# Every third step's edge rows and every fourth step's mask made in the first edge pass, and the softmax's copies on ScalarE

## The reference

```
# weighted layer
neighbor = segment_sum(weight * x[src], dst)
out = x @ W1.T + b1 + (neighbor + neighbor * x) @ W2.T + b2
x = layernorm(x + normalize(leaky_relu(out, 0.2)))
# attention layer: two convolutions of 4 heads of 64 channels, relu between them
q, k, v = h @ Wq + bq, h @ Wk + bk, h @ Wv + bv
e = edge_attr @ We
logits = sum_c(q[dst] * (k[src] + e)) / sqrt(64)
a = softmax of logits over the edges of one dst
conv = segment_sum((v[src] + e) * a, dst) + h @ Ws + bs
x = layernorm(x + conv2(relu(conv1(x))))
```

## Time and profile before

| what | value |
|---|---|
| median of 3 runs | 4665.41 us |
| the profiled execution, its own time | 4668.24 us |
| its span, first to last instruction | 4666.5 us |
| mean granted TensorE clock | 0.981 of full |
| TensorE (PE) busy | 4159.3 us, 89% |
| VectorE (DVE) busy | 3873.8 us, 83% |
| ScalarE (ACT) busy | 2969.4 us, 64% |
| GpSimd (POOL) busy | 3113.8 us, 67% |
| DMA, mean | 214 GB/s, 996.73 MB |

### The profile page before, as it was taken

One profiled execution on the slowest core, in us unless ns is written; L12 is line 12 of the kernel. 1 busy time (PEld: TensorE's weight loads), 2 busy tenths in 40 slices (PEclk: granted clock), 3 DMA queues, 4 the chain that ended last, 5 costly groups with the idle time before them and its releaser, 6 DMA issues. The chain is left out here.

```text
span 4666.5 us, 107658 instructions
## 1 busy us (share of the span) xinstructions
PE 4159.3 (89%) x17694; PEld 3201.7 (69%) x17694; DVE 3873.8 (83%) x21108; ACT 2969.4 (64%) x10607; POOL 3113.8 (67%) x2996
## 2 busy tenths in 40 slices
PE   2888888888978999999999998979999999999989
PEld 2766666665546777777777775557777777777755
DVE  4655555556869999999999998879999999999987
ACT  1111111112316999999999996129999999999970
POOL 6677777770038777777777772188777877787730
PEclk9999999998999999999999999999999999999999
DMA  4666666664558888888888884578888888888844
GB/s 117 189 195 193 193 195 193 193 187 132 167 174 258 241 245 248 244 244 243 245 248 243 248 241 127 181 227 243 243 239 241 239 243 243 240 241 242 241 124 155
DMA packets 663064, 996.73 MB, mean 214 GB/s; under 512 B 99667, under 2 KB 489690, under 8 KB 662407
## 3 DMA queue, kind: packets, MB, share of 16 engines
q0 software_dynamic: 171408, 540.40, 39.3%
q1 hardware_dynamic: 491000, 449.44, 31.8%
HBM read 870.01 MB, written 119.44 MB: 212 GB/s over the span
## 5 line engine op out<-in xcount | busy, mean ns | idle before, releaser
L1303 POOL DMA_INDIRECT e_kv<-kv,src x1664 | 1633.9, 982 | 599.1 <-DVE e_kvj L1418 289.5
L1558 ACT ACTIVATE e_vals<-e_kvj,e_ex 128x65 f32<-128x65 f32 x6572 | 1723.2, 334 | 1.3 <-PE e_sum L1366 1.3
L1325 PE MATMUL e_q<-q,e_pick 128*128 x3328 | 1035.1, 392 | 146.4 <-DVE e_logit L1430 111.4
L1430 DVE CUSTOM_DVE_ANT_0 e_kvj<-e_kvj,e_q 128x64 f32<-128x64 f32 x6656 | 1062.5, 214 | 7.6 <-PE e_q L1325 2.7
L1366 PE MATMUL e_sum<-e_vals,e_mask 128*128 128x260 f32 x3328 | 1033.6, 393 | 28.7 <-ACT e_vals L1558 15.3
L152 POOL DMA_INDIRECT e_x<-x_rows,e_src x783 | 745.1, 952 | 263.6 <-issue 174.0
L1418 DVE TENSOR_TENSOR e_kvj<-e_kv,e_e 128x512 f32<-128x512 f32 x1248 | 845.5, 678 | 44.3 <-DMA e_kv<-kv,src 39.2
L1325 PEld LDWEIGHTS e_q<-q,e_pick 128*128 128x128 f32 x3328 | 594.1, 191 | 376.4 <-issue 302.0
L1315 PE MATMUL e_e<-e_we,e_ea 112*128 112x256 f32 x2496 | 749.6, 381 | 15.3 <-DMA e_ea<-attr_tiles 14.6
L1316 PE MATMUL e_e<-e_we,e_ea 112*128 112x256 f32 x2496 | 743.5, 379 | 0.0
L1512 DVE TENSOR_TENSOR acc<-acc,e_sum 128x260 f32 x1664 | 693.8, 417 | 32.2 <-PE e_sum L1366 9.3
(11 more groups left out here) (221 smaller groups left out, 3979.2 us busy)
## 6 DMA issues: line engine op xcount, KB each, us to landing
e_ea<-attr_tiles SPq DMA_DIRECT2D x1248, 112.0 KB
edges<-q SPq DMA_DIRECT2D x208, 256.0 KB, 3.1
e_spots<-locals SPq DMA_DIRECT2D x416, 128.0 KB
e_made<-edges SPq DMA_DIRECT2D x416, 128.0 KB
e_kv<-kv,src POOLq DMA_INDIRECT x1664
kv<-n_proj_rows SPq DMA_DIRECT2D x98, 256.0 KB
q<-attr_tiles SPq DMA_DIRECT2D x208, 112.0 KB
n_x<-x_rows SPq DMA_DIRECT2D x98, 128.0 KB
```

The costliest lines, as they stand in the source:

```text
L1303: e.indirect_dma_start(out=kv[:, u, :], out_offset=None, **rows_of(kv_rows, k["src"][:, i:i + 1])).then_inc(kv_got[u], 16)
L1325: e.matmul(pe_q[i % 2][:, 0:D], pick[:, c, at:at + P], rows, start=True, stop=True).then_inc(q_done, 1)
L1430: dot = e.tensor_tensor_reduce(kvj[:, i % 2, h, 0:C], kvj[:, i % 2, h, 0:C], pe_q[i % 2][:, hs], 1.0, 0.0, ALU.mult, ALU.add, logit[:, j % ...
L1558: by_weight = e.activation(vals[:, n % R, h * HV:(h + 1) * HV], kvj[:, 2 + n % NV, h, :], ACT.Copy, scale=ex[:, b % 2, h, r:r + 1])
```

## The change

e0 makes edge rows at every third step (`TRIO` = 3, 277 times for 208) and also, at every fourth step, the plain mask that e1 and e2 need, on ScalarE, and stores it in a DRAM table `masks` (208 of 64 KB). e1 and e2 read the made rows at every third step, make `e` themselves at two of three, and load the mask at every fourth step (below `LATE`) into two buffers instead of making it. To have room, NE is 4 for 5. The copies of pieces 3 and 5 go from VectorE to ScalarE, where they stand at pieces 2 and 4.

```diff
+TRIO = 3
...
+class PlainMasks:
+    def make(self, e, c):
+        n = c * QUAD
+        if c:
+            e.wait_ge(self.made, c)
+        e.activation(self.apart, self.k["iota"][:], ACT.Square, bias=self.k["local"][:, n:n + 1], scale=-1.0).then_inc(self.apart_done, 1)
+        e.wait_ge(self.apart_done, c + 1)
+        if c >= 2:
+            e.wait_ge(self.stored[c % 2], 16 * (c // 2))
+        e.activation(self.masks[c % 2], self.apart, ACT.Relu, bias=self.k["one"][:, 0:1], scale=-1.0).then_inc(self.made, 1)
+
+    def store(self, e, c):
+        e.wait_ge(self.made, c + 1)
+        e.dma_start(self.table[c * P:(c + 1) * P, :], self.masks[c % 2]).then_inc(self.stored[c % 2], 16)
...
             for i in range(T):
-                c = i // QUAD
-                if i % QUAD == 0 and c + edges.AHEAD - 1 < s.quads:
+                c = i // TRIO
+                if i % TRIO == 0 and c + edges.AHEAD - 1 < s.trios:
                     ahead = c + edges.AHEAD - 1
-                    edges.load(e, ahead, tile.at(QUAD * ahead + QUAD - 1))
-                if i % QUAD == 2 and c:
+                    edges.load(e, ahead, tile.at(TRIO * ahead + TRIO - 1))
+                if i % TRIO == 2 and c:
                     edges.store(e, c - 1)
+                if i % QUAD == 2:
+                    plain.store(e, i // QUAD)
...
-                if i % QUAD == 1:
-                    edges.multiply(e, i // QUAD)
+                if i % TRIO == 1:
+                    edges.multiply(e, i // TRIO)
...
         @block.scalar
         def _(e):
-            for c in range(s.quads):
-                edges.copy(e, c)
+            for i in range(T):
+                if i % QUAD == 1:
+                    plain.make(e, i // QUAD)
+                if i % TRIO == 2:
+                    edges.copy(e, i // TRIO)
...
-    NV, NG, NE, R = LAG + 2, 6, 5, 4
+    NV, NG, NE, R = LAG + 2, 6, 4, 4
...
+        def mask_kept(n):
+            return n < LATE and n % QUAD == 0
+        def masks_before(n):
+            return n - -(-n // QUAD)
+        def mask_of(n):
+            return plain[:, n // QUAD % 2, :] if mask_kept(n) else mask[:, n % R, :]
         def mask_made(e, n):
-            if n < LATE:
-                e.wait_ge(masked, n + 1)
+            if mask_kept(n):
+                c = n // QUAD
+                e.wait_ge(plain_got[c % 2], 16 * (c // 2 + 1))
+            elif n < LATE:
+                e.wait_ge(masked, masks_before(n) + 1)
...
+                def load_mask(c):
+                    if c >= 2:
+                        e.wait_ge(summed, (c - 2) * QUAD + 1)
+                    e.dma_start(plain[:, c % 2, :], masks_made[c * P:(c + 1) * P, :]).then_inc(plain_got[c % 2], 16)
...
-                    if at == QUAD - 1 and c + 1 < s.quads:
+                    if at == TRIO - 1 and c + 1 < s.trios:
                         load_made(c + 1)
+                    n = i - LAG + 3
+                    if n >= 0 and mask_kept(n):
+                        load_mask(n // QUAD)
...
-                        last, before = 7 * PACE + 1, 5 * PACE + 1
+                        last, before = 7 * PACE + 1, 4 * PACE + 1
...
                     elif step == 3:
-                        e.wait_ge(ends_up, j + 1)
+                        e.wait_ge(rows_in, 2 * j + 2)
                         if j:
-                            e.wait_ge(outs_done, j)
                             e.wait_ge(across, j)
                             e.wait_ge(history, j)
-                        e.tensor_copy(by_head(row_f[:]), by_head(small[0:1, 0:RW])).then_inc(rows_in, 1)
-                        e.tensor_copy(by_head(row_b[:]), by_head(small[0:1, RW:2 * RW])).then_inc(rows_in, 1)
-                        e.wait_ge(rows_in, 2 * j + 2)
...
                     elif step == 5:
-                        e.wait_ge(across, j + 1)
-                        e.tensor_copy(ends[:], back[:, P:P + 2]).then_inc(ends_down, 1)
...
-                        if n < LATE:
-                            if n:
-                                e.wait_ge(masked, n)
+                        if n < LATE and not mask_kept(n):
+                            if masks_before(n):
+                                e.wait_ge(masked, masks_before(n))
                             e.activation(apart[:], k["iota"][:], ACT.Square, bias=k["local"][:, n:n + 1],
...
+                    elif step == 2:
+                        e.wait_ge(ends_up, j + 1)
+                        if j:
+                            e.wait_ge(outs_done, j)
+                        e.activation(by_head(row_f[:]), by_head(small[0:1, 0:RW]), ACT.Copy).then_inc(rows_in, 1)
+                        e.activation(by_head(row_b[:]), by_head(small[0:1, RW:2 * RW]), ACT.Copy).then_inc(rows_in, 1)
+                    elif step == 4:
+                        e.wait_ge(across, j + 1)
+                        if j:
+                            e.wait_ge(mx_done, j)
+                        e.activation(ends[:], back[:, P:P + 2], ACT.Copy).then_inc(ends_down, 1)
```

64 lines of the change are left out of this document (38 added, 26 removed).

## The result

| what | before | after |
|---|---|---|
| median | 4669.27 us (7 runs, 4661.03 to 4674.04) | 4652.98 us (7 runs, 4650.67 to 4656.75) |
| ratio after to before | | 0.9968, 95% interval 0.9957 to 0.9979 |
| the profiled execution, its span | 4668.24, 4666.5 us | 4656.75, 4654.4 us |

The change makes the kernel faster by 0.3%: little, but the interval stays under 1. The forecast was 4582, or 83 to 87 us less; it came to 16. The result also lies above the upper end of my range, 4645.

The account below looks back on a forecast made before the run. ScalarE was taken to bound e2, VectorE a hair behind, both sharing e1. From 4668.2 us, minus 97 (attention passes) plus 14 (e0) gave 4585; the median being 2.8 lower, 4582, range 4530 to 4645.

Parts of the forecast that it names:

- The reading of the bound: In e2 ScalarE bounds at 44.9 us a batch, VectorE a hair behind; in e1 the two share it.
- I take a third left: Attention passes: VectorE's idle 1.7 (e1) and 1.1 us (e2) a batch falls to 0.5 and 0.3.
- POOL at 1.62 a step, 42.2 a batch: Attention passes: POOL's need, from 1.25 us a gather and 2.74 where a pick stands between two.
- VectorE's busy time: Attention passes: falls by 0.65 us a batch, to 43.8 in e1 and 43.4 in e2.
- The copies: Softmax in e1 and e2: moving three copies saves VectorE 0.65 us a batch and costs ScalarE 0.77.
- The masks and made rows: Attention passes: masks save ScalarE 4.7 us a batch; made rows save TensorE 1.9.
- SP and transfers: Attention passes: masks add 0.10 us a step of transfers; DMA share reaches 0.92 in e1, 0.90 in e2.
- e0: Weighted pass: added products hidden under POOL's gathers except at both ends, 7.2 us each, +14 us; bounds 3 and 40.
- Transfers cap the pace: Rival, attention passes: transfers capped at 260 GB/s, e1 gains only 0.9 us a batch, time 4609; chance 0.15.
- transfers are the limit today: Rival, attention passes: transfers are already full at 245 GB/s, so added bytes cost time, 4773; chance 0.07.
- It does nothing: Rival, whole kernel: masks or copies end up waited for at the same places, 4665; chance 0.03.
- VectorE's waits stay: Rival, attention passes: VectorE is late for its own reasons, only the copies are gained, 4639; chance 0.13.

Follow-up runs that it names:

- half pick: POOL's pick cut to half its width, result not computed: 4605.5 us (0.9870) in the changed kernel, 4639.2 us (0.9947) in the kernel before.
- pick per three steps: The changed kernel with POOL's pick made for three steps at a time instead of four: 4656.8 us, ratio 0.9982.
- the two kernels without overlaps: The changed kernel with picks made per three steps (4656.8 us), or with made rows back at every fourth step (4652.0 us).

## Why the prediction was wrong

**The reading of the bound.** ScalarE as the bound of e2, at 44.9 us a batch, isn't shown. The copies alone give ScalarE work and take it from VectorE, and e2 gets faster by 9 us; my expectation had named a gain of over 10 us in all as the sign that VectorE was the bound. That e2 then stands at 44.8 us a batch (the line that adds starts 580 times in 1000 us), with ScalarE at 0.978, agrees in number. What the runs do show is that the engines stand so close together in e2 that relieving one brings 14 or 16 us and both 55. What the text never compared was how far below the bound the next engine stood, by means.

**The step that failed: "I take a third left", VectorE's idle time of 0.5 us a batch in e1 and 0.3 in e2.** Measured are 0.034 x 45.8 = 1.6 and 0.017 x 44.7 = 0.8, nearly the old 1.7 and 1.1. I had put this time down to ScalarE and TensorE alone. In e2 this goes back to a number beside the sum, what POOL needs; in e1 the cause stays open.

**In e2: POOL at 1.62 a step, 42.2 a batch.** I took 1.25 and 2.74 from rows of single intervals. They are near the shortest that occur: the gather behind a pick takes 1.33 to the next, and one gather in the same stretch of the trace took 1.23 instead of 0.95. In the kernel before, POOL's true slack in e2 was 37 us in 1000 (worked out above), so its need was 963/576 = 1.67 a step, 43.5 a batch. After the change the gathers and picks are longer by 0.022 and 0.090/4 = 0.023, and 1.67 + 0.045 = 1.715 a step is 44.6 a batch, against 44.7 measured. So POOL became e2's bound within 0.3 us of the old one, with VectorE (43.9 busy) 0.8 below it. The half pick brings e2 to 43.7, partly by relieving VectorE too, and the pick per three steps relieves VectorE alone and brings next to nothing. The stretch by overlap is a part of it at most: in the two kernels without overlaps the gathers stay at 1.007 and 1.018, for which I have no cause, and e2 gains little.

**In e1**, where 46 of the 75 us are missing, the idle time stayed as well, and its cause is open; what the waits say is at the end of this section.

**VectorE's busy time** came out at 44.2 and 43.9 for 43.8 and 43.4; the made adds, 8.7 a batch and each longer by 0.040, are 0.35 of that.

**The copies.** Right in sign, and the only part that pays: 30 us (copies moved back) and 28 us (copies alone) for 40 by my sum of 2 x 0.65 x 30.4. ScalarE's price was set too high (0.77 for some 0.3), and that VectorE's shorter chain gives ScalarE back its wait at the exponential was not seen. That new waits on TensorE cost nothing is neither confirmed nor refuted.

**The masks and made rows.** Forecast as the relief of the bound, 57 us in the passes (97 - 40); over the copies alone they bring 1 us there (+4 and -5) and cost 14 in e0. ScalarE did come down, to 0.872 x 45.8 = 39.9 busy a batch, for the 41.0 forecast as its need; the room isn't used, because POOL and VectorE, and in e1 something else, stand right behind it. "One buffer of attributes fewer" was priced at nothing; in e1's window TensorE and its weight loads now wait 4.4 and 9.3 us for attributes, which they didn't before.

**SP and transfers.** Forecast shares 0.92 and 0.90, measured 0.87 and 0.85. Part of that is the pace; by share times pace the new transfers cost 0.87 x 1.761 - 0.83 x 1.773 = 0.06 and 0.85 x 1.718 - 0.81 x 1.736 = 0.05 a step for my 0.10. "The tightest resource" was wrong here: the run with fewer bytes changed nothing. (The added bytes come to 17.7 kB a step, not 17.6.) For these masks I had an estimate of 0.24 a step from the table of the Trainium skill (DMA: Bandwidth & Descriptors, Bandwidth), whose rows are for transfers issued from GpSimd, while SP loads the masks. The trace doesn't bear the estimate out: the whole change of share is worth 0.05 to 0.06.

**e0.** Right: +10 for +14, with 400 gathers in 500 us as before, and POOL's stop, as I had worked out (26), in the timeline:

```profile
148.79 0.94 POOL L153 DMA_INDIRECT e_x<-x_rows,e_src  x1 [25.65 <-PE e_sum L631]
```

**The rivals.** "Transfers cap the pace" and "transfers are the limit today" fall by the run with fewer bytes. "It does nothing", 4665, came nearest in time, but the interval of the ratio rules it out, and the copies do bring something. "VectorE's waits stay", 4639, was the nearest in mechanism (POOL was named there among others), but it still credited the change with the copies' whole 40 us and saw no lengthening. I gave it 0.13; its argument "POOL already waits for VectorE 89.5 us" I read as POOL following with room, where 52 of the 89.5 were the gap that stands between any two gathers.

**What stays open**: what holds e1 at 45.5 to 46.3 us a batch in nearly every kernel on the first kind of chip. It isn't the amount of bytes (fewer bytes: the same) and not POOL's width (half pick: 8 us). In e1's window POOL waits for VectorE 78.7 us, 174 times, so 26.5 over the gaps. VectorE's largest waits there are these:

```profile
DVE e_block_rows L469 <- PE e_back L461: 13.2, 28, 0.9
DVE e_kvj L1478 <- issue: 7.8, 12, 1.6
```

and one of SP's own is this:

```profile
SPq L473 <- DVE e_block_rows L469: 140.8, 34, 5.8
```

VectorE's first wait, for the skip product, was 15.4 before; its second, on nothing that the profile names, is new. The two together are 21 of the 33.9 us that VectorE is idle there, and my 0.5 a batch had left room for 11 in all. The row of SP goes with late attributes: SP stands at the store of each skip product until VectorE has reached it, up to 5.8 us, and loads nothing meanwhile; of the 30 times that TensorE or its weight loads wait more than 0.15 us before an edge product in e1, 28 lie within 14 us behind such a store, and the stores are 30 us apart. With five buffers, in the kernel before, there were 7 such waits. So the skip product is the likeliest cause of a part of what e1 lacks, by VectorE's wait and by SP's order, but taking it out of e1 or moving its store wasn't tried.

## What to carry to other kernels

Price every engine that is near the bound by its mean cycle over the stretch, the gap that it always has included (busy time plus waits, less only what a wait has over that gap), before you credit a relief of the bound: here the next ones stood 3% behind and took over, and in e2 relief for two at once brought more than the two reliefs apart. When two engines disturb each other, look at where in the instruction they meet, and not only how often. And try the parts of a change alone: the three copies are worth more without the rest, by 11 us and without its 68 MB of transfers.

## What was unexpected of the hardware

- A POOL compare of 128x512 and a VectorE add that reads both operands from on-chip buffers lengthen each other: 1.61 to 1.78 us and 0.68 to 0.80 on average, single ones to 2.69 and 1.28. Only an add that begins less than 0.6 us into the pick, or before it, does this (100 of after's 179: 1.93 and 0.90); one that begins later changes nothing (1.60 and 0.68). An add that takes one operand from TensorE's result doesn't change (0.677). The Trainium skill (Advanced Engine Details and Errata, GPSIMD Details) names the conflict of the two engines for VectorE instructions with two SBUF inputs, without a price; these rows agree and give one.
- Small ScalarE instructions (1x104, 0.23 us each) start 0.13 to 0.14 us apart.
- Chips differ. On the second kind the kernel before takes 5081 us for 4667. In e0 a gather comes every 1.51 us there in the changed kernel, and every 1.48 with the copies alone, for 1.25; the sign of this change is the other there. The trace of the changed kernel on it, 500 us of e0, to be set beside the third window of after above:

```profile
500.00:1000.00 500.00, 409.49 (x1632) 324.74 (x1630) 222.50 (x683) 117.38 (x274) 313.57 (x331) 0.93 0.64 192
```

331 gathers for 400, at a granted clock of 0.93 for 0.97 and a DMA share of 0.64 for 0.77.
